# Layer 1 of a graph network kernel: half of the dense products from float32 to three float32r terms, with a subtraction on VectorE

## The reference, cut to what matters

```python
h = relu(layernorm(x))
xn = _bn(h, g0, be0)
h = _bn(relu(_gcn_conv(xn, src, dst, edge_weight, W1, b1, n)), g1, be1)
h = _bn(relu(_graph_conv(h, src, dst, edge_weight, Wrel2, brel2, Wroot2, n)), g2, be2)
h = _bn(relu(_graph_conv(h, src, dst, edge_weight, Wrel3, brel3, Wroot3, n)), g3, be3)
return x + h
```

## Time and profile before

| | |
|---|---|
| device time, median of 3 runs | 3447.38 us (3444.28 to 3447.8) |
| the profiled execution's own time | 3449.69 us |
| its span in the trace | 3447.9 us |
| TensorE matmul busy | 2844.8 us, 83% |
| VectorE busy | 2603.7 us, 76% |
| ScalarE busy | 2310.8 us, 67% |
| granted TensorE clock, mean | 0.913 of full rate |

### The profile page before, as it was taken

One profiled execution on the slowest core, in us unless ns is written; L12 is line 12 of the kernel. 1 busy time (PEld: TensorE's weight loads), 2 busy tenths in 40 slices (PEclk: granted clock), 3 DMA queues, 4 the chain that ended last, 5 costly groups with the idle time before them and its releaser, 6 DMA issues. The chain is left out here.

```text
span 3447.9 us, 51737 instructions
## 1 busy us (share of the span) xinstructions
PE 2844.8 (83%) x12445; PEld 1955.9 (57%) x12445; DVE 2603.7 (76%) x5601; ACT 2310.8 (67%) x4070; POOL 1310.1 (38%) x1196
## 2 busy tenths in 40 slices
PE   3666499999997899999999999699999999554542
PEld 2666355555554677777777777555555555443432
DVE  6999388888888788888888888678888888533332
ACT  4999377777775688888888887466666667333331
POOL 1657656556551421111211110132222221266576
PEclk9999799999998999999999999899999999655555
DMA  5999499999996799999999999589999998799997
GB/s 193 344 344 328 133 333 345 339 342 340 337 339 253 271 345 344 346 347 344 344 347 346 344 348 329 185 295 339 340 339 341 340 339 316 288 365 363 381 357 227
DMA packets 335138, 1106.81 MB, mean 321 GB/s; under 512 B 54569, under 2 KB 102210, under 8 KB 285906
## 3 DMA queue, kind: packets, MB, share of 16 engines
q1 hardware_dynamic: 211964, 905.05, 71.8%
q0 software_dynamic: 62656, 77.70, 10.0%
q10 hardware_dynamic: 60438, 123.18, 9.9%
HBM read 599.13 MB, written 498.21 MB: 318 GB/s over the span
## 5 line engine op out<-in xcount | busy, mean ns | idle before, releaser
L1265 POOL DMA_INDIRECT l_ed_gathered<-agg_rows,pos_cols x392 | 399.8, 1020 | 1419.1 <-PE l_ps L1277 699.8
L1162 DVE TENSOR_TENSOR dense_tiles<-dense_tiles,l_dn_top 128x512 fp32r<-128x512 f32 x784 | 501.7, 688 | 235.1 <-ACT l_dn_top L1130 235.1
L1103 PE MATMUL l_ps<-l_dn_top,wroot_top 128*128 128x512 f32 x1176 | 502.6, 427 | 73.2 <-ACT l_dn_ho L1117 43.3
L1130 ACT ACTIVATE l_dn_top<-dense_tiles 128x512 fp32r<-128x512 f32 x784 | 447.8, 623 | 32.1 <-issue 31.7
L1103 PE MATMUL l_ps<-l_dn_top,wroot_rest 128*128 128x512 f32 x1176 | 468.3, 398 | 0.0
L1103 PE MATMUL l_ps<-dense_tiles,wroot_top 128*128 128x512 f32 x1176 | 463.0, 394 | 0.0
L745 PE MATMUL l_ps<-l_dn_columns,w_fold 128*128 128x512 f32 x784 | 382.0, 610 | 31.0 <-ACT l_dn_ho L780 31.0
L1117 ACT ACTIVATE l_dn_ho<-l_ps,bias_fold 128x512 f32<-128x512 f32 x392 | 263.4, 685 | 160.0 <-PE l_ps L1103 159.5
L1733 PE MATMUL out_ps<-ident,dense_tiles 128*128 128x128 f32 x784 | 185.6, 415 | 208.6 <-ACT dense_tiles L1720 208.6
L1103 PEld LDWEIGHTS l_ps<-l_dn_top,wroot_top 128*128 128x128 f32 x1176 | 222.6, 189 | 183.3 <-ACT l_dn_ho L1117 64.2
L1749 DVE TENSOR_TENSOR out_od_ot<-out_ps,x_tiles 128x512 f32<-128x512 f32 x196 | 134.7, 691 | 246.9 <-PE out_ps L1733 242.8
(11 more groups left out here) (247 smaller groups left out, 6245.9 us busy)
## 6 DMA issues: line engine op xcount, KB each, us to landing
h_dense<-l_dn_ho SPq DMA_DIRECT2D x188, 1024.0 KB, 10.8
dense_tiles<-h_dense SPq DMA_DIRECT2D x188, 1024.0 KB, 8.6
l_dn_rows<-h_rows SPq DMA_DIRECT2D x98, 520.0 KB, 6.9
h_rows<-norm_ln_ho SPq DMA_DIRECT2D x97, 520.0 KB, 4.3
h_dst<-l_ed_ho SPq DMA_DIRECT2D x98, 512.0 KB, 6.3
l_ed_hd<-h_dst ACTq DMA_DIRECT2D x98, 512.0 KB
norm_ln_x<-in_x SPq DMA_DIRECT2D x97, 512.0 KB, 5.4
x_tiles<-in_x SPq DMA_DIRECT2D x97, 512.0 KB, 15.3
```

What stands on the lines that cost most here:

```text
L1103: ins = pe.matmul(o, a, b, start=t == 0, stop=t == len(terms) - 1)
L1130: act.activation(top[:, j % 2, k, cc], hi[:, j, k, cc], ACT.Copy).then_inc(tp[j], 1)
L1162: dve.tensor_tensor(rest[:, j, k, cc], hi[:, j, k, cc], top[:, j % 2, k, cc].bitcast(FP), ALU.subtract).then_inc(spl[j], 1)
L1265: pool.indirect_dma_start(tg[:, j, g, :], None, tab[n - 1][:, :], bass.IndirectOffsetOnAxis(ap=pos_c[:, t:t + 1], axis=0)).then_inc(gat[j] ...
```

## The change

The columns of half 1 are kept in two float32r parts: top, which ScalarE writes when it evicts the half, and rest, which VectorE makes by subtracting top from the same PSUM bank. The products u1 and u3 become three float32r matmuls each (top by top, rest by top, top by rest of the weight). TensorE waits for rest before u1, and before it turns the next tile's half 1 into bank 1. The fold at the end of norm makes the two parts of the weight.

```diff
+        w1f_top, w1f_rest = front_sb("w1_fold_top", [C, H1], FR), front_sb("w1_fold_rest", [C, H1], FR)
...
-            hc, ho = ph.sb("dn_columns", [C, 2, W]), ph.sb("dn_ho", [C, NS, 2, W])
+            hc, ho = ph.sb("dn_columns", [C, 2, CW]), ph.sb("dn_ho", [C, NS, 2, W])
+            c_top, c_rest = ph.sb("dn_column_top", [C, 2, CW], FR), ph.sb("dn_column_rest", [C, 2, CW], FR)
+            cr = ph.slots("dn_column_rest", NS)
...
-                        if m == 0:
-                            wait_use(pe, ev[j], i, CH, c + 1)
+                        if m == 0 and c == 0:
+                            wait_use(pe, ev[j], i, CH, 1)
+                        elif m == 0:
+                            wait_use(pe, cr[j], i)
...
-                        pe.matmul(ps[:, 2 + u % 2, 0:CW], wfold[1][:, 0, m * C:(m + 1) * C], hc[:, j % 2, c * CW:(c + 1) * CW],
-                                  start=True, stop=True).then_inc(mm[j], 1)
+                        mc = slice(m * C, (m + 1) * C)
+                        terms = [(wfold[1][:, 0, mc], hc[:, j % 2, :])]
+                        if c == 1:
+                            terms = [(w1f_top[:, mc], c_top[:, j % 2, :]), (w1f_top[:, mc], c_rest[:, j % 2, :]), (w1f_rest[:, mc], c_top[:, j % 2, :])]
+                        for t, (a, b) in enumerate(terms):
+                            ins = pe.matmul(ps[:, 2 + u % 2, 0:CW], a, b, start=t == 0, stop=t == len(terms) - 1)
+                        ins.then_inc(mm[j], 1)
...
                     for c in range(CH):
-                        wait_use(pe, ev[j1], i1, CH, c + 1)
+                        if c == 0:
+                            wait_use(pe, ev[j1], i1, CH, 1)
+                        else:
+                            wait_use(pe, cr[j1], i1)
...
-                        act.activation(hc[:, j % 2, c * CW:(c + 1) * CW], ps[:, c, 0:CW], ACT.Copy).then_inc(ev[j], 1)
+                        act.activation((hc, c_top)[c][:, j % 2, :], ps[:, c, 0:CW], ACT.Copy).then_inc(ev[j], 1)
...
-                return NS, [(2, mask), (6, statistics)], end
+                def column_rest(i, j):
+                    i2, j2 = before(i, j, 2, NS)
+                    wait_use(dve, mm[j2], i2, per)
+                    wait_use(dve, ev[j], i, CH, 2)
+                    dve.tensor_tensor(c_rest[:, j % 2, :], ps[:, 1, 0:CW], c_top[:, j % 2, :].bitcast(FP), ALU.subtract).then_inc(cr[j], 1)
+
+                return NS, [(4, column_rest), (2, mask), (6, statistics)], end
...
+                if n == 0:
+                    link(dve.tensor_copy(w1f_top[:, :], folded[:, 0, :]))
+                    link(dve.tensor_tensor(w1f_rest[:, :], folded[:, 0, :], w1f_top[:, :].bitcast(FP), ALU.subtract))
```

## The result

The changed kernel takes 3667.79 us (median of 5, 3664.02 to 3673.66), the kernel before beside it 3446.91 (5, 3444.28 to 3447.8): a ratio of 1.0643, 95% interval 1.0629 to 1.0658. It is 221 us slower. 3680 was forecast, in a range of 3590 to 3750. The profiled execution took 3672.38 us, its span 3670.5.

A forecast was written before the change was run, and what follows sets the result against it. TensorE was the fullest engine in layer 1, VectorE close behind; the change would close a ring of waits. On 3449.69 us, +174 +5 +1 +54 = +234 gave 3684; the median, 2.3 lower, 3681, stated as 3680, range 3590 to 3750.

The forecast's parts named there:

- The alignment of the rounds: Layer 1: VectorE is already at the next round's edge work when half 1 is evicted, 5.8 us too late for it.
- the ring: Layer 1, each round: spread, u0, u1, relu 0, relu 1, half 1, subtraction, mask, statistics, L1011 or L997, next spread.
- The ring's length: Layer 1: rounds of 8.50 and 9.06 us, a chunk of 17.56 against 14.01.
- Its sum: Layer 1: 3.55 us more per chunk x 49 chunks = 174 us more.
- The aggregate: One-off L689, two of 4.87 us: costs TensorE its whole 9.70 in place of 4.47, +5 us.
- The clock: Layer 1: TensorE's idle gaps of 3.5 and 1.2 us lower its clock; 1.3 us in some 42 of 49 chunks, +54.
- ScalarE: Eviction of half 1 writing float32r in place of float32: 0.62 us again, so zero cost.
- TensorE's saving: u1 and u3: 31 us less TensorE work, of which at most 16 us (98 x 0.16) could reach the end.
- The subtraction: VectorE, one 128x512 operation per tile: taken as 0.61 us in a queue.
- The fold's: Two more 128x256 operations in the fold before layer 1: between 0 and 1.4 us, taken as 1.
- Rivals 3 and 4: Layer 1: VectorE merely full, 3427 to 3471 us (0.05); or TensorE bound and the kernel faster, 3431 us (0.04).
- rival 4: Layer 1: TensorE is the bound, u3 shorter by 0.16 us per tile, VectorE's gather wait swallows the subtraction: 3431 us, 0.04.

The follow-up runs named there:

- e1: Changed kernel with the subtraction moved behind mask and statistics in VectorE's list: 3429.68 us, 0.9946 of the kernel before.
- e5: Changed kernel with the subtraction one round later (lag 5 in place of 4), still ahead of mask and statistics: 3478.06 us, 1.008.
- e6: Changed kernel with both column halves ahead of relu 0 and 1 in ScalarE's list: 3516.54 us, 1.0198.
- e3: Changed kernel with the subtraction done twice, the second waiting for the first: 3749.06 us, 1.0872.
- e10: Changed kernel with relu 0 and 1 ahead of both column halves in ScalarE's list: 3740.19 us, 1.0834.
- e4: Changed kernel with half 1's four turns repeated seven times for even j, 24 more transposes in TensorE's idle stretch: 3614.69 us, 1.0481.
- e9: Changed kernel with 12 ordinary float32 identity products ahead of the turns of half 1, for even j: 3614.32 us, 1.0486.
- e2: Changed kernel without the subtraction; TensorE waits for the eviction alone and the middle term reads top for rest: 3430.86 us, 0.9947.

## Why the prediction was right, point by point

- **The alignment of the rounds** and the ring that follows from it hold: VectorE waits ahead of 97 of 98 subtractions and TensorE ahead of 96 of 98 spreads, where it waited ahead of two before. e1, e5 and e6 open the ring at three different places, and e3 and e10 put known lengths into it, which come back at full clock as 1.46 us a chunk for 1.48 and 1.00 for 0.94.
- **The ring's length** was put at 17.56 us a chunk; e4 shows 17.62. This is not two errors that cancel: the two rounds were put at 8.50 and 9.06 and take 8.55 and 9.08 (the spreads below and the one at 818.69), and the piece from the start of the spread to the end of half 1 was put at 3.38 and takes 3.39 (801.06 to 804.45). TensorE and ScalarE in e4:

```profile
801.06 0.62 PE L929 MATMUL l_ps<-ident,l_ed_coef 128*128 128x128 f32 x4 [0.61 <-DVE l_ed_dst L1030]
...
809.61 0.65 PE L929 MATMUL l_ps<-ident,l_ed_coef 128*128 128x128 f32 x4 [0.93 <-DVE l_ed_message L1016]
```

```profile
803.86 0.59 ACT L781 ACTIVATE l_dn_column_top<-l_ps 128x512 fp32r<-128x512 f32 x1
```

- **Its sum** was put at 174 us, for all 49 chunks. With the 5 and 1 that makes 180; e4 stands 167 above the kernel before (3614.69 against 3448.01 beside it). Most of the 13 too many are the step "x 49": the first chunks are not slower in the ring. The third L987 starts at 411.87 in the kernel before, the third L1006 at 412.94 in the changed one and at 409.89 in e4. From there to the last one, 46 steps, the kernel before takes 649.43 us and e4 813.48, 164 more, or 3.57 a chunk. So the size per chunk was right, and three chunks, 10 of the 13 us, were counted too many; e4's earlier third chunk is 2 more. The last us is not accounted for.
- **The aggregate** L689 (L690 now) was put at +5 on the ground that TensorE would now bear all of it. TensorE's gap there is 11.16 us, against 4.47 before, and 0.8 of it is the usual one of an odd round (49.7 less 11.2 over 47), so 5.9 more:

```profile
1298.45 1.12 PE L929 MATMUL l_ps<-ident,l_ed_coef 128*128 128x128 f32 x4 [11.16 <-DVE l_ed_message L1016]
```

- **The clock** was put at 54 us; e4 and e9 give 53 by taking it away (3667.79 less 3614.69 and 3614.32, with the kernel before at 3446.91, 3448.01 and 3448.6 beside them). That it comes so close is in part luck, for its factors were off in opposite directions. 42 chunks at 1.3 us were expected; the measured average is 18.79 - 17.62 = 1.17 us over all steady chunks, of which 25 in 27 have a low stretch. The piece wholly at the low level was put at 4.85 us and takes 5.28 (808.28 to 813.56), 1.9 more than at full clock and not 1.5; but in most chunks only part of it is low. TensorE's gaps were put at 3.5 and 1.2 us and are 3.2 and 0.8 (means without the longest). The Trainium skill, "TensorE: Matmul & The Clock Gate", section "Why this matters for your kernels", warns of idle gaps between bursts of matmuls; the trace agrees, with 3.2 us gaps and a clock of 0.50 behind them, and e4 and e9 show the gap as a cause. The clock also fell after the gap of 2.10 us, which is shorter than those that the page warns of.
- **ScalarE** at zero: L781 with float32r takes 590 ns, with float32 596.
- **TensorE's saving**: 16 us and no more, which e2 confirms with 17.
- **The subtraction**: 691 ns long, 0.60 from its start to the mask's (813.60 to 814.20), 0.61 taken.
- **The fold's** 1 us is below what these runs can tell.
- Rivals 3 and 4 would have been right only if half 1 were out when VectorE came to it. e1 shows that world: VectorE at 97.7%, and 3430 us, where rival 4 had put 3431.

What remains open: why VectorE is late in e5. The wait may run over the gathers (35.4 us of waits at L1006), which was not taken apart.

## What to carry to other kernels

In a kernel whose engines run fixed lists, price a new operation by where it stands, not by its length: ask what it waits for, what is queued behind it, and whether that queue leads back to what it waits for. Here 0.69 us per tile in one place of the list cost 237 us (the changed kernel against e2, which has no subtraction), and two places further down nothing. Look for a lead of one engine over another before putting a wait ahead of the work that makes the lead. And try the cheap reordering first: moving two evictions on ScalarE gave more than the split of the products.

## What the runs showed of the hardware that I had not expected

Adding work made the kernel faster: 24 transposes per chunk in an idle stretch of TensorE took 53 us off, and 12 float32 products in the same place took the same, with the clock at 1.00 in place of 0.91.
